# Row maxima of an attention kernel: key-difference units in every second turn, and no plain copies of the other units

## What is computed

```python
Q = _lora_linear(x, Wq, bq, Aq, Bq).reshape(N, S, HEADS, HEAD_DIM)
K = _lora_linear(x, Wk, bk, Ak, Bk).reshape(N, S, HEADS, HEAD_DIM)
V = _lora_linear(x, Wv, bv, Av, Bv).reshape(N, S, HEADS, HEAD_DIM)
energy = jnp.einsum('nqhd,nkhd->nhqk', Q, K) / jnp.sqrt(jnp.float32(HEAD_DIM))
attn = jax.nn.softmax(energy, axis=-1)
out = jnp.einsum('nhqk,nkhd->nqhd', attn, V).reshape(N, S, EMBED)
```

## Time and profile before

| | before |
|---|---|
| median of 3 runs | 1810.09 us |
| span of the profiled execution, first to last instruction | 1807.2 us |
| TensorE busy (share of the span) | 1788.2 us (99%) |
| VectorE busy | 1489.3 us (82%) |
| ScalarE busy | 1471.9 us (81%) |
| GpSimd busy | 357.0 us (20%) |
| mean granted TensorE clock | 0.996 |

### The profile page before, as it was taken

The page is one execution under the profiler, slowest core; times in us unless marked ns, Lnnn a source line. Parts: engine busy times, 40 slices in busy tenths (PEclk is TensorE's granted clock), DMA queues, the critical chain, the costliest instruction groups (busy, mean ns, idle before and its releaser), DMA issues.

```text
span 1807.2 us, 35352 instructions
## 1 busy us (share of the span) xinstructions
PE 1788.2 (99%) x13143; PEld 809.3 (45%) x13144; DVE 1489.3 (82%) x2716; ACT 1471.9 (81%) x1908; POOL 357.0 (20%) x441
## 2 busy tenths in 40 slices
PE   9999999999999999999999999999999999999997
PEld 5533333333333333333333333333326555699996
DVE  6889999999999999999999999999935422355553
ACT  6559999999999999999999999999997411254442
POOL 6655020020000000000000200001010177233333
PEclk9999999999999999999999999999999999999998
DMA  7534131232111121111313211133124733322221
GB/s 232 151 112 120 34 89 45 82 103 60 42 45 34 43 58 59 47 34 45 91 46 98 59 42 44 42 72 86 33 69 165 286 97 117 120 81 65 67 68 42
DMA packets 87294, 145.71 MB, mean 81 GB/s; under 512 B 18692, under 2 KB 53765, under 8 KB 87020
## 3 DMA queue, kind: packets, MB, share of 16 engines
q1 hardware_dynamic: 78220, 119.22, 22.2%
q0 software_dynamic: 7936, 23.10, 4.0%
q10 hardware_dynamic: 992, 1.44, 0.2%
HBM read 93.85 MB, written 50.36 MB: 80 GB/s over the span
## 4 chain that ended last, share of the span: by engine, by line
PE 84%; DVE 6%; DMA 5%; ACT 2%; POOL 1%; issue 1%; SPq 1%; POOLq 0%; DVEq 0%; ACTq 0%
PE ps L1218 25%; PE ps L1206 22%; PE ps L1149 14%; PE ps L1985 8%; DVE mx L1266 4%; PE ps L2008 4%; PE ps L727 3%; DMA sc_x<-n_rows 2%; DMA sorted_in<-sc_x,slot 2%; PE ps L1551 2%; PE ps L746 1%; ACT prob L1338 1%; PE ps L1521 1%; DVE mx L1277 1%; PE ps L1858 1%
## 5 line engine op out<-in xcount | busy, mean ns | idle before, releaser
L1266 DVE TENSOR_REDUCE mx<-ps 128x1 f32<-128x512 f32 x1588 | 1004.6, 684 | 11.6 <-PE ps L1149 7.4
L1338 ACT ACTIVATE prob<-ps 128x1024 f32<-128x1024 f32 x1024 | 992.8, 1021 | 3.3 <-issue 1.6
L1149 PE MATMUL ps<-k_high,q_high 64*128 64x512 bf16 x2048 | 577.5, 382 | 0.9 <-DVE mx L1266 0.2
L1218 PE MATMUL ps<-prob,vs 128*32 128x512 f32 x4096 | 545.5, 605 | 0.2 <-ACT head_out_sb L1344 0.2
L1206 PE MATMUL ps<-q_low,k_low 34*128 34x512 bf16 x2048 | 490.6, 377 | 0.0
L1206 PE MATMUL ps<-q_high,k_high 64*128 64x512 bf16 x2048 | 490.0, 376 | 0.5 <-ACT prob L1338 0.3
L1149 PEld LDWEIGHTS ps<-k_high,q_high 64*128 64x128 bf16 x2048 | 143.2, 93 | 547.1 <-DVE mx L1266 444.3
L1277 DVE TENSOR_REDUCE mx<-unit_sb 128x1 f32<-128x512 f32 x460 | 310.8, 676 | 0.0
L1317 ACT COPY unit_sb<-ps 128x512 f32<-128x512 f32 x460 | 269.6, 586 | 5.5 <-PE ps L1149 2.0
L1206 PEld LDWEIGHTS ps<-q_low,k_low 34*128 34x128 bf16 x2048 | 143.2, 94 | 118.7
L1367 POOL CAST mb<-turned_sb 16x128 bf16<-16x128 f32 x32 | 9.0, 283 | 826.4 <-ACT turned_sb L1324 814.9
(11 more groups left out here) (173 smaller groups left out, 1445.3 us busy)
## 6 DMA issues: line engine op xcount, KB each, us to landing
k_high<-qk_parts SPq DMA_DIRECT2D x126, 128.0 KB, 2.7
qk_parts<-parts SPq DMA_DIRECT2D x32, 384.0 KB, 3.0
k_low<-qk_parts SPq DMA_DIRECT2D x128, 64.0 KB
q_high<-qk_parts SPq DMA_DIRECT2D x126, 64.0 KB, 2.4
head_out<-head_out_sb SPq DMA_DIRECT2D x31, 256.0 KB, 2.2
sorted_in<-zero_row POOLq DMA_DIRECT2D x13, 390.0 KB, 4.6
xs<-sorted_in SPq DMA_DIRECT2D x39, 130.0 KB
q_low<-qk_parts SPq DMA_DIRECT2D x128, 32.0 KB
```

Of the source, the lines that this page charges most:

```text
L1149: pe.matmul(ps[:, ring.bank((n, m, u)), :], q_high[p][mine, t * P:(t + 1) * P], k_high[p][mine, c * CH:(c + 1) * CH], start=True, stop=Tru ...
L1218: mm = pe.matmul(ps[32 * j:32 * j + 32, 7, :], vs[buf(h)][:, kt, :], prob[:, (kt + 1) % 2, j * CH:(j + 1) * CH], start=(kt == 0), stop=(kt ...
L1266: dve.tensor_reduce(mx[n % 2][:, at, c:c + 1], ps[:, ring.bank(what), :], AX.X, ALU.max).then_inc(s_ring, 1)
L1338: act.activation(prob[:, (kt + 1) % 2, :].rearrange("p (u c n) -> p u c n", u=2, c=2)[:, :, half, :], ps[:, bank:bank + 2, :], ACT.Exp).th ...
```

## The change

Every second C becomes a key-difference unit. For c = 1 and u = 0 (`steps_of`, the same heads as before) the unit's keys are not block 1 but the difference of block 1 and block 2 of the keys, so that the product is s1 - s2. ScalarE takes its positive part (Relu) into one SBUF buffer. For c = 2 and u = 0 (`folded`) VectorE adds that to the bank of block 2 and takes the maximum of the sum in one instruction: s2 + max(s1 - s2, 0) is the larger of the two. The other C units (c = 3) are no longer copied: VectorE reduces them from the bank, as it does at m = 11. The difference of the keys is made by GpSimd in the projection (first batch) and in head 7 (second batch), stored, and loaded by two more DMAs per head. To make room, the shared weights wuT and wdT are loaded in head 9 instead of at the start of attention, and the last expert's gate weights after the merge. The diff, cut to its core:

```diff
-def carried(n, m, u):
-    return u == 0 and m % 2 == 1 and m != LEAD - 1 and (n >= 2 or n == 1 and m >= LEAD)
+def steps_of(n, m, u):
+    return u == 0 and m % CPB == STEP and (n >= 2 or n == 1 and m >= LEAD)
+def folded(n, m, u):
+    return u == 0 and m % CPB == STEP + 1 and steps_of(n, m - 1, u)
...
+                if kept(g, o) and g >= CPB:
+                    act.wait_ge(s_kstepst, 16 * HALF)
+                act.activation(full(g, o)[:], ps[:, bank, :], ACT.Identity, bias=bqk[:, o:o + 1], scale=scale)
...
+        def key_steps(pool, step, half):
+            step(pool.tensor_tensor(k_from[half][:], k_from[half][:], k_to[half][:], ALU.subtract))
+            step(pool.tensor_copy(step_parts[half][:, 0, :], k_from[half][:]))
+            pool.tensor_tensor(step_parts[half][:, 1, :], k_from[half][:], step_parts[half][:, 0, :],
+                               ALU.subtract).then_inc(s_kstep, 1)
...
+                if n in STEPS_BEHIND:
+                    key_steps(pool, step, STEPS_BEHIND.index(n))
...
             stack_low(sp, (0, 0), 1)
+            for half in range(HALF):
+                store_key_steps(sp, 0, half)
...
             for u in range(2):
                 stack_high(eng, h, u)
+            load_key_steps(eng, h)
...
-            pe.matmul(ps[:, ring.bank((n, m, u)), :], q_high[p][mine, t * P:(t + 1) * P],
-                      k_high[p][mine, c * CH:(c + 1) * CH], start=True, stop=True).then_inc(s_max, 1)
+            keys = k_high[p][mine, c * CH:(c + 1) * CH]
+            if steps_of(n, m, u):
+                pe.wait_ge(s_kstep_in, 32 * n)
+                keys = k_step[n % 2][mine, :]
+            pe.matmul(ps[:, ring.bank((n, m, u)), :], q_high[p][mine, t * P:(t + 1) * P], keys,
+                      start=True, stop=True).then_inc(s_max, 1)
...
+                if steps_of(*what):
                     continue
+                bank, largest = ps[:, ring.bank(what), :], mx[n % 2][:, u * HT + t, c:c + 1]
                 dve.wait_ge(s_max, ring.made(what))
+                if folded(*what):
+                    dve.wait_ge(s_turned, ring.taken((n, m - 1, u)))
+                    dve.tensor_tensor_reduce(step_sb[:], bank, step_sb[:], 1.0, LOWEST, ALU.add, ALU.max,
+                                             largest).then_inc(s_ring, 1)
+                else:
+                    dve.tensor_reduce(largest, bank, AX.X, ALU.max).then_inc(s_ring, 1)
...
-                    if m % 2 == 0:
-                        reduce_carried(dve, n, m - 1)
...
             act.wait_ge(s_max, ring.made(what))
-            wait(act, s_carried, k - NCOPY + 1)
-            act.copy(unit_sb[k % NCOPY][:], ps[:, ring.bank(what), :]).then_inc(s_turned, 1)
+            if k:
+                act.wait_ge(s_ring, step_folded[k - 1])
+            act.activation(step_sb[:], bank, ACT.Relu).then_inc(s_turned, 1)
...
             merged(sp)
+            sp.dma_start(rgT[:, E - 1:E], io["rgT"][:, E - 1:E]).then_inc(s_expert_late, 16)
             for e in range(E):
                 sp.dma_start(ruT[:, e:e + 1], io["ruT"][:, e:e + 1]).then_inc(s_expert_late, 16)
```

More of the change, by code:

```diff
@@ L69 @@
 SLOTS = 6
-NCOPY = 2
+STEP = 1
+LOWEST = -3.0e38
 BESIDE = LEAD
@@ L90, in wait, with earlier @@
         eng.wait_ge(semaphore, n)
-def carried(n, m, u):
-    return u == 0 and m % 2 == 1 and m != LEAD - 1 and (n >= 2 or n == 1 and m >= LEAD)
-def carried_before(n, m):
-    return sum(carried(k, j, 0) for k in range(n + 1) for j in range(PAIRS if k < n else m))
+def steps_of(n, m, u):
+    return u == 0 and m % CPB == STEP and (n >= 2 or n == 1 and m >= LEAD)
+def folded(n, m, u):
+    return u == 0 and m % CPB == STEP + 1 and steps_of(n, m - 1, u)
+def earlier(kind, n, m):
+    return sum(kind(k, j, 0) for k in range(n + 1) for j in range(PAIRS if k < n else m))
 class Region:
@@ L562, in unit, with kept, full @@
             return 2 * g + o // 2 if g < CPB and o % 2 == 0 else EARLY + 2 * g + o // 2 if g < CPB else UQ * g + o
+        def kept(g, o):
+            return o >= 2 and g % CPB in (STEP, STEP + 1)
+        def full(g, o):
+            return (k_from, k_to)[g % CPB - STEP][o - 2] if kept(g, o) else qf[unit(g, o) % UQ]
+        UNITS_AT = {unit(g, o): (g, o) for g in range(NCH) for o in range(UQ)}
         def adapt(pe, first):
@@ L818, in take @@
                 n = unit(g, o)
-                slot, bank, scale = n % UQ, 2 + n % 2, 0.25 if o < 2 else 1.0
+                bank, scale = 2 + n % 2, 0.25 if o < 2 else 1.0
                 act.wait_ge(s_unit, n + 1)
                 act.wait_ge(s_qf_free, n + 1)
-                act.activation(qf[slot][:], ps[:, bank, :], ACT.Identity, bias=bqk[:, o:o + 1], scale=scale)
+                if kept(g, o) and g >= CPB:
+                    act.wait_ge(s_kstepst, 16 * HALF)
+                act.activation(full(g, o)[:], ps[:, bank, :], ACT.Identity, bias=bqk[:, o:o + 1], scale=scale)
                 act.wait_ge(s_parts[n % SLOTS], 16 * (n // SLOTS + 1))
@@ L905, in fill_ones, with store_key_steps, load_key_steps @@
                 step(pool.memset(k_low[p][u * HROWS + LROWS:u * HROWS + LROWS + 2, :], 1.0))
+        def key_steps(pool, step, half):
[3 more added lines that the diff above has]
+                               ALU.subtract).then_inc(s_kstep, 1)
+        def store_key_steps(sp, b, half):
+            sp.wait_ge(s_kstep, HALF * b + half + 1)
+            at = slice(b * D + half * P, b * D + (half + 1) * P)
+            sp.dma_start(step_dram[:, at, :].rearrange("s c t -> c s t"), step_parts[half][:]).then_inc(s_kstepst, 16)
+        def load_key_steps(sp, h):
+            n = num(h)
+            sp.wait_ge(s_kstepst, 16 * HALF * (n // H + 1))
+            wait(sp, s_kstep_in, 32 * (n - 1))
+            mine = slice(n * DH, (n + 1) * DH)
+            for part in range(2):
+                sp.dma_start(k_step[n % 2][part * LROWS:(part + 1) * LROWS, :],
+                             step_dram[part:part + 1].to_broadcast([2, B * D, CH])[:, mine, :]
+                             .rearrange("a d t -> d a t")).then_inc(s_kstep_in, 16)
         def project_gpsimd(pool, step):
@@ L1077, in prepare @@
                         sp.dma_start(xg_dram[c], xg[c][:]).then_inc(s_xgst, 16)
+                if n == XB_AT + 4:
+                    for half in range(HALF):
+                        store_key_steps(sp, 1, half)
+                if n == XB_AT + 5:
+                    sp.wait_ge(s_kstepst, 16 * HALF * B)
+                    for dst, name in ((wuT, "wuT"), (wdT, "wdT")):
+                        sp.dma_start(dst[:], io[name]).then_inc(s_shared, 16)
                 if n == XB_AT + 1:
@@ L1261, in reduce_pair @@
                 what = (n, m, u)
-                at = u * HT + t
-                if carried(*what):
+                if steps_of(*what):
                     continue
+                bank, largest = ps[:, ring.bank(what), :], mx[n % 2][:, u * HT + t, c:c + 1]
                 dve.wait_ge(s_max, ring.made(what))
[L1266 to L1278, removed]
+                if folded(*what):
[4 more added lines that the diff above has]
+                    dve.tensor_reduce(largest, bank, AX.X, ALU.max).then_inc(s_ring, 1)
         def negate(dve, n):
             dve.wait_ge(s_ring, ring.taken((n, PAIRS - 1, 1)))
-            wait(dve, s_carried, carried_before(n, PAIRS))
             dve.tensor_reduce(mneg[:], mx[n % 2][:], AX.X, ALU.max, negate=True).then_inc(s_neg, 1)
+            if n < 2:
+                dve.wait_ge(s_neg, n + 1)
+                dve.memset(mx[n][:, 0:HT, STEP:STEP + 1], LOWEST)
         def attend_vector(dve, step):
@@ L1297, in attend_vector @@
                         invert(dve, 1, m // 8)
-            reduce_carried(dve, NH - 1, PAIRS - 1)
             negate(dve, NH - 1)
             invert(dve, 2, 0)
+        step_folded = [ring.taken((n, m + 1, 0)) for n in range(NH) for m in range(PAIRS) if steps_of(n, m, 0)]
         def carry(act, g):
@@ L1311, in carry @@
                 return
-            what, k = (who, first + 1, 0), carried_before(who, first + 1)
-            if not carried(*what):
+            what = (who, first + 1, 0)
+            bank = ps[:, ring.bank(what), :]
+            if not steps_of(*what):
                 return
+            k = earlier(steps_of, who, first + 1)
             act.wait_ge(s_max, ring.made(what))
-            wait(act, s_carried, k - NCOPY + 1)
-            act.copy(unit_sb[k % NCOPY][:], ps[:, ring.bank(what), :]).then_inc(s_turned, 1)
+            if k:
+                act.wait_ge(s_ring, step_folded[k - 1])
+            act.activation(step_sb[:], bank, ACT.Relu).then_inc(s_turned, 1)
         def take_turned(act, n):
@@ L1398, in following @@
                 i, u = divmod(n + 1 - NB, NB)
-                if i < E and u == 0:
+                if i < E - 1 and u == 0:
                     pool.dma_start(rgT[:, bass.ds(i, 1)], io["rgT"][:, bass.ds(i, 1)]).then_inc(s_expert, 16)
@@ L1427, in attend_gpsimd @@
```

(4 more changed lines are left out.)

37 lines of the change are left out of this document (24 added, 13 removed).

## The result

The changed kernel is slower: median 1823.5 us of 4 runs (1822.59 to 1824.37) against 1810.01 us of the kernel before (4 runs), ratio 1.0074, 95% interval 1.0063 to 1.0086: a small difference, but clear of no change. The direction and the mechanism of the main term, (a), came out; its size did not, and a smaller term, (g), came out too high as well. The profiled execution took 1822.59 us.

A forecast was written before the change was run, and what follows sets the result against it. The prediction took TensorE as the bound, with VectorE merely keeping up. Its terms, 23.5 + 0.5 - 1.3 + 0.5 + 1.5 = +24.7 us on 1810.1, gave 1834.8 us, range 1824 to 1851 us.

The forecast's parts named there:

- (a): C units with c = 3 reduced by VectorE from their bank make B's load wait: 214 x 0.11 = 23.5 us.
- (g): After the merge, one more expert load before the 16 makes the routing rows later: +1.5 us (0 to 2).
- The bound: In a common turn of attention, 2.41 us, TensorE sets the length and VectorE merely keeps up.
- VectorE was the bound: Rival: in attention TensorE follows VectorE's starts, two turns cost 4.3 instead of 4.8, so 1688 us; chance 0.07.
- (b): C units with c = 1 stay with ScalarE, a Relu for a copy: 0 us.
- (c): VectorE's fold takes about the 0.688 us of the nearest row: 0.5 us, from turns with the transpose.
- (d): VectorE's spared reduction gives something back only at the 12 reciprocals in heads 20 and 27: -1.3 us.
- (e): ScalarE loses 215 copies, and TensorE doesn't wait for it: 0 us.
- (f): In the projection, GpSimd's six added operations delay ScalarE's take of unit 22: 0 to 3 us, 0.5 taken.
- a swallowed wait: Rival: B's wait for VectorE to free C's bank costs nothing, leaving +1, 1811 us; chance 0.07.
- a late Relu: Rival: ScalarE's Relu on C units with c = 1 comes later than the copy, 1847 to 1850 us; chance 0.09.
- a table load: Rival: ScalarE's Relu needs another table than the exponential, two loads in each of 245 turns, about 2400 us; chance 0.01.

The follow-up runs named there:

- e3: The changed kernel with ScalarE copying the C units with c = 3 (not m = 11) as before; key differences and folds stay: 1804.24 us, ratio 0.9990.
- e1: The kernel before with only the C units with c = 3 moved to VectorE, no key differences: 1827.03 us, ratio 1.0116.
- e4: The kernel before with only the last expert's gate weights loaded behind the merge: 1806.12 us, ratio 1.0001.
- e2: On top of e1, VectorE reduces the copied unit of c = 1 only behind C and D with c = 3: 1935.04 us, ratio 1.0713.
- e5: The changed kernel with an extra VectorE reduction of 256 constant elements right in front of each C with c = 3: 1825.62 us, ratio 1.0082.
- e8: The changed kernel as it is, run once more as yardstick on the chip of the runs beside it: 1824.46 us, ratio 1.0075.
- e6: The changed kernel with an extra VectorE reduction of 512 constant elements right in front of each C with c = 3: 1854.89 us, ratio 1.0240.

## Why the prediction was wrong, point by point

**The bound.** Right. TensorE gives the turn its length: with one reduction in eight gone no whole turn with units of maxima beside it is shorter than 2.40 us, and both other engines only gained idle time. The rival "VectorE was the bound" falls.

**(a) C units with c = 3 on VectorE, 214 x 0.11 = 23.5 us.** This is the step that failed, by the size of its term. Mechanism, place and count came out: the turns alternate, B's load waits for VectorE in every second one. The price was taken from m = 11 with the words that VectorE starts on C "at once when it is complete" and, among the rivals, that "VectorE is not behind either". It was behind, by 0.04 us: the row in front of 715.40 is the reduction of a copied unit, which the change takes away. The step read the start of C's reduction and not what stood in front of it. What the runs showed in its place: 0.08 us per turn, 16.3 us in all (e3 against the changed kernel); the term's own range, 0.09 to 0.12, did not reach down to it. With a reduction still in front of C the price is the predicted one: 2.52 us per turn in e1. The 31 turns at m = 11 lost the same 0.03 us each, 0.9 us that no part of the sum had; with the reciprocals they are the 2.1 us of e3.

**(b) The Relu, 0; (c) the fold, 0.5 us.** Right in what matters: e3 has both and its turns are 2.41. The Relu's row is 597 ns against 597 taken, the fold's 691 against 688. Of the half microsecond for the turns with the transpose nothing is to be seen; the reading of the accumulator is a row of its own of 0.08 us, and the next reduction starts at its start (716.12). The rule of the Trainium skill (VectorE: DVE Perf Modes, section "Two Vector instructions with no wait between them"), that an instruction with an accumulator output is two, agrees with these rows, and it changes the sum by nothing.

**(d) The reciprocals, -1.3 us.** About right: e3 gives 2.1 us in attention with 0.9 of it from m = 11, which leaves 1.2. Three turns show it: 3.14, 2.86 and 2.70 us in heads 19, 18 and 25 of the kernel before, 2.62, 2.49 and 2.49 in e3. The mechanism was read from a row; that a third of the bound was the right share was a guess that came out.

**(e) ScalarE's copies, 0.** Right.

**(f) The projection, +0.5 us.** Nothing was lost there: the first transpose is at 114.0 us instead of 115.0. That one microsecond is not the change's either: e1 and e4, whose projection is that of the kernel before, have it at 113.9 and 114.0. In the profiled execution of the kernel before, TensorE's granted clock is 0.81 on the mean between 4 and 13 us, which makes 3.4 of the 9 us at the lower of its two levels (1.2 GHz); in that of the changed kernel it is 1.00, the higher level (2.4 GHz) throughout. Between 6 and 8 us, before it fell, the engine had been busy for 1.46 us (1.79 in the changed kernel, where it did not fall); what made it fall no run shows. The stretches, with the busy time of each engine, then the clock:

```profile
4.00:13.00 9.00, 8.05 (x47) 6.31 (x46) 5.40 (x21) 2.78 (x5) 2.98 (x2) 0.81 1.04 346
```
```profile
4.00:13.00 9.00, 8.29 (x52) 6.04 (x51) 6.32 (x24) 2.89 (x5) 2.97 (x2) 1.00 1.05 341
```

e2, at 115.0, loses its microsecond elsewhere, at a clock of 1.00: TensorE waits 0.98 us at 41 us.

**(g) The expert load, +1.5 us.** Too high. The routing rows start about 1.0 us later behind the last transpose: 110.8 to 111.6 us in the seven profiles with the late load, 110.0 to 110.6 in the three without it. But the chain behind them reaches TensorE in some executions only: the wait of the earlier trace rows is missing in the changed kernel's profile and in e3, e4 and e5, and is back in e8 with 0.71. The term took a wait that comes and goes for the fixed state of that stage. By the medians of e4 it was worth 0; what it is worth on average stays open within that run's interval.

The sum as it should have been: 214 x 0.08 = 17, less 0.9 for m = 11 and 1.2 for the reciprocals, about 15 us; the transposes show 14.2, the medians 13.5. Of the 24.7 predicted, (a) was 6.4 to 7.2 too high, (g) most of its 1.5, (c) and (f) 0.5 each, and the 0.9 were missing.

**The rivals.** Kept out by the traces: VectorE as the bound, a swallowed wait, a late Relu, a table load. The last was the one place where a page decided and no row did: the Trainium skill (ScalarE: Activation LUTs, section "Table sets: the hidden batching unit") has Relu in every set, and the trace agrees, with 245 Relus between exponentials and no load.

## What to carry to other kernels

Before a stall seen in one turn is multiplied, look at what stands in front of the instruction that caused it: if the change removes that too, the stall shrinks (here from 0.11 to 0.08 us, and the forecast with it by more than a quarter). Where a bank is wanted back a fixed time after it is filled, relieving the slower reader is worth nothing unless the release of every bank stays in time; with 0.04 us to spare, which engine frees it matters more than how busy that engine is. A wait of half a microsecond, seen once in one profile, does not say that its chain is always exposed: here it was there in four profiled executions of ten.

## What the runs showed of the hardware that was not expected

An extra reduction of 256 elements, 245 times, costs nothing measurable when it ends by the time the unit is complete (e5), and one of 512, after which the unit is started 0.15 us late, costs 0.13 us in seven turns of eight (e6). The fold reads one operand from PSUM and one from SBUF, writes 512 columns and an accumulator, and takes 0.691 us, against 0.685 for a plain reduction of a bank; the next instruction starts together with the accumulator's read of 0.08 us, 0.62 after the fold. And in e1 two kinds of turn, 2.49 and 2.52 us, live side by side, and all that the trace shows to set them apart is whether TensorE's transpose had given VectorE 0.2 us to catch up.
